# Eigenvector stage of a graph kernel: z on TensorE, the tangents' sum on GpSimd, the basis copy and each reflection's squares on ScalarE

## The reference, cut to what matters

```python
L_norm = d_inv_sqrt[:, None] * (jnp.diag(deg) - A) * d_inv_sqrt[None, :]
_, U = jnp.linalg.eigh(L_norm)
agg = jnp.einsum('mn,bnd->bmd', U.T, features)
h = jax.nn.relu(agg @ W1 + b1)
out = h @ W2 + b2
return jnp.einsum('nm,bmd->bnd', U, out)
```

## Time and profile before

| | |
|---|---|
| median of 3 runs | 1087.52 us |
| the profiled execution | 1086.33 us |
| its span | 1084.5 us |
| granted TensorE clock, mean | 0.881 of full speed |
| eigenvector stage | 38 to about 455 us, over a third of the span |

### The profile page before, as it was taken

How to read it: one execution, slowest core, us unless ns; L and a number is a source line. 1 busy time by engine, 2 the same in 40 slices (tenths; PEclk the granted TensorE clock), 3 DMA queues, 4 the chain that set the end, 5 groups by cost and what they waited for, 6 DMA issues and landing times.

```text
span 1084.5 us, 13522 instructions
## 1 busy us (share of the span) xinstructions
PE 933.4 (86%) x4093; PEld 631.0 (58%) x4093; DVE 659.7 (61%) x2237; ACT 569.2 (52%) x1460; POOL 158.8 (15%) x390
## 2 busy tenths in 40 slices
PE   4788867878866676699999999999999998899995
PEld 3555545545555565466788877886444465554443
DVE  4667676654757788357635598533544455553686
ACT  0555543754534665338655345534965565664456
POOL 0122222311322222100000000000011111110055
PEclk9699985977956555589999999999999999999998
DMA  9100000000000000000000000000000000000014
GB/s 261 32 1 1 1 1 0 1 1 1 1 1 1 1 1 1 1 1 1 1 1 1 1 2 1 2 1 1 1 1 0 0 1 1 1 0 1 0 40 116
DMA packets 14328, 12.99 MB, mean 12 GB/s; under 512 B 897, under 2 KB 11057, under 8 KB 14257
## 3 DMA queue, kind: packets, MB, share of 16 engines
q1 hardware_dynamic: 14018, 11.98, 3.9%
q10 hardware_dynamic: 238, 0.16, 0.1%
HBM read 7.89 MB, written 4.19 MB: 11 GB/s over the span
## 4 chain that ended last, share of the span: by engine, by line
PE 71%; DVE 18%; ACT 5%; issue 3%; POOL 1%; DMA 0%; DVEq 0%; SPq 0%; POOLq 0%; ACTq 0%
PE bank L884 15%; PE bank L908 9%; PE bank L805 3%; PE bank L750 3%; PE bank L740 3%; PE bank L764 3%; PE bank L795 3%; PE bank L467 2%; PE bank L573 2%; PE bank L704 2%; PE bank L460 1%; PE bank L715 1%; PE bank L871 1%; PE bank L813 1%; PE bank L863 1%
## 5 line engine op out<-in xcount | busy, mean ns | idle before, releaser
L1330 ACT ACTIVATE hid_t<-bank,gate_b 128x512 f32<-128x512 f32 (+1 forms) x252 | 150.8, 631 | 67.8 <-PE bank L908 66.7
L908 PE MATMUL bank<-ms,w_t 128*128 128x512 f32 (+1 forms) x288 | 112.9, 536 | 6.8 <-DVE ms L2062 6.8
L884 PE MATMUL bank<-hid_t,w_t 128*128 128x336 f32 (+1 forms) x296 | 106.4, 506 | 1.1 <-DVE x L2066 1.1
L1422 POOL COPY hid_t<-feat_t 128x1008 f32<-128x1008 f32 (+1 forms) x12 | 27.9, 2328 | 499.3 <-DVE feat_t L2058 499.3
L884 PE MATMUL bank<-feat_t,w_t 128*128 128x512 f32 x208 | 93.1, 603 | 0.0
L908 PEld LDWEIGHTS bank<-ms,w_t 128*128 128x128 f32 x288 | 54.6, 193 | 56.5 <-issue 34.3
L884 PEld LDWEIGHTS bank<-hid_t,w_t 128*128 128x128 f32 x296 | 56.2, 191 | 46.0 <-issue 26.2
L1124 ACT ACTIVATE hs<-bank,con 128x1 f32<-128x1 f32 x62 | 16.2, 261 | 102.3 <-PE bank L574 102.3
L1337 ACT ACTIVATE hid_t<-hid_t 128x512 f32<-128x512 f32 (+1 forms) x72 | 41.8, 580 | 52.3 <-DVE hid_t L2044 27.6
L884 PEld LDWEIGHTS bank<-feat_t,w_t 128*128 128x128 f32 x208 | 39.2, 189 | 50.9 <-issue 46.7
L982 ACT ACTIVATE x<-x,perm 128x128 f32<-128x128 f32 x128 | 52.3, 482 | 2.6 <-DVE perm L1461 2.6
(11 more groups left out here) (443 smaller groups left out, 2166.7 us busy)
## 6 DMA issues: line engine op xcount, KB each, us to landing
out<-x SPq DMA_DIRECT2D x16, 256.0 KB, 2.6
con<-in_constants SPq DMA_DIRECT2D x1, 449.0 KB, 3.2
hid_t<-in_L_gnn_W SPq DMA_DIRECT2D x2, 128.0 KB, 3.7
e_int<-in_L_gnn_src ACTq DMA_DIRECT2D x1, 128.0 KB
l_w<-in_L_gnn_W SPq DMA_DIRECT2D x2, 64.0 KB
wg<-in_L_gnn_Wg SPq DMA_DIRECT2D x2, 64.0 KB
adj_n<-in_adj SPq DMA_DIRECT2D x1, 64.0 KB, 3.7
hid_t<-in_L_gnn_W_lin SPq DMA_DIRECT2D x1, 64.0 KB, 3.3
```

Source lines behind the costliest of these rows:

```text
L884: return mm(bank[4 * u + BANK_OF[g]][:, 0:w], w_t[:, WB_IH + 4 * (it.p - 1) + g, :], lstm_x(n), start=True, stop=(it.k == 0))
L908: mm(bank[4 * u + BANK_OF[g]][:, 0:w], w_t[:, WB_HH + 4 * (it.p - 1) + g, :], lstm_h_of(it.chain)[:, 0:w], start=False, stop=True).then_in ...
L1330: f(dst[:, 0:w], bank[4 * u + BANK_OF[g]][:, 0:w], ACT.Tanh if g == G_G else ACT.Sigmoid, bias=gate_b[:, 4 * (it.p - 1) + g:4 * (it.p - 1) ...
```

## The change

Five things of the eigenvector stage move to another engine:

- z = row * sigma + y was VectorE's L1689. Now `pe_rows` leaves the accumulation of y open and a new `pe_z` adds sigma times the row with a product of a 1 x 1 weight; VectorE reads z out of PSUM. `pe_z` waits for the copied row (`h_a_row`) and for GpSimd's sigma (`h_sigma`).
- The sum of the tangents (L1637, 128 x 128) goes from VectorE to GpSimd (`pool_den`), behind GpSimd's scalars for h1.
- The copy of v_nat (`dve_v`, L1669) goes from VectorE to ScalarE, in front of the copy of v_t.
- The sum of squares of each reflection (L1720) goes from VectorE to ScalarE (`act_vector`), in front of the root.
- The square of the lead (L1115) goes from ScalarE to GpSimd.

On ScalarE, `act_vector` of h2 moves ahead of `act_y`. At the end of the program three semaphores of the final norm are replaced by counts of semaphores that exist already; the work there is the same.

```diff
+            def pe_z(h):
+                if h is None or h == HALF - 1:
+                    return
+                k = h + 1
+                pe.wait_ge(s["h_a_row"], h + 1)
+                pe.wait_ge(s["h_sigma"], h + 1)
+                mm(h_y[:, k:P], scalar(h, SIGMA), a_row[h % 2][:, k:P], start=False, stop=True).then_inc(s["h_rows"], 1)
...
                 pe_rows(h0)
                 pe_w(i)
+                pe_z(h0)
                 beside(h0)
...
                 pe_rows(h1)
+                pe_z(h1)
                 beside(h1)
...
                 pe_rows(h2)
                 pe_turn(i)
+                pe_z(h2)
                 beside(h2)
...
                 pe_rows(h3)
                 pe_y2(i)
+                pe_z(h3)
                 beside(h3)
...
             def act_vt(i, polished):
...
+                act.wait_ge(s["j_v"], i + before + polished + 1)
+                t = f(v_nat, j_v, ACT.Copy)
...
             def act_vector(h):
...
-                link(f(scalar(h, LEAD2), lead, ACT.Square, scale=2.0))
+                f(square_row[:, h + 2:P], vp_row[h % 4][:, 0, h + 2:P], ACT.Square, accum_out=scalar(h, SUM)).then_inc(s["h_sum"], 1)
                 act.wait_ge(s["h_sum"], h + 1)
+                act.wait_ge(s["h_lead2"], h + 1)
                 f(scalar(h, NORM2), scalar(h, SUM), ACT.Sqrt, scale=4.0, bias=scalar(h, LEAD2)).then_inc(s["h_norm"], 1)
...
-                act_matrix(h2)
+                act_step(h2)
                 act_y(i)
-                if h2 is not None:
-                    act_vector(h2 + 1)
...
+                pool.tensor_scalar(scalar(h, LEAD2), lead, lead, 4.0, ALU.mult, ALU.mult).then_inc(s["h_lead2"], 1)
...
+            def pool_den(i):
+                pool.wait_ge(s["j_hyp"], i + 1)
+                pool.tensor_tensor(jt, jabs, jhyp, ALU.add).then_inc(s["j_den"], 1)
...
             def dve_tangents(i):
-                dve.wait_ge(s["j_hyp"], i + 1)
-                link(tt(jt, jabs, jhyp, ALU.add))
+                dve.wait_ge(s["j_den"], i + 1)
...
-                    link(stt(z_row[:, k:P], a_row[h % 2][:, k:P], scalar(h, SIGMA), h_y[:, k:P], ALU.mult, ALU.add))
...
-                squares(h + 1)
```

More of the change, by code:

```diff
@@ L62 @@
 TILES = 2 * PAIRS
+FIN_BASE = 2 * TILES + PAIRS
 AT_TURNED, AT_PRODUCTS, AT_LEVEL, AT_Q = (1, 11), (2, 12), (3, 13), (8, 19)
@@ L259, in graph_layers @@
         c_col = hs[:, 23:24]
+        square_row = s_flt[0:1, :]
         kept, solved, wy_t, wy_n = src_1h, dst_1h[0:HALF, 0, :], dst_1h[:, 1, :], rot[0:HALF, :]
@@ L331, in graph_layers @@
             x_ready ln_var ln_std ln_scale l0_added deg_in deg_std bn_var bn_std eig_start
[L332 removed]
+            j_w j_w_sb j_vw j_off j_d j_osq j_dif j_dsq j_sign j_sum j_hyp j_den j_t j_root j_b j_bt j_x j_y j_v1 j_y_sb j_v1_sb
             j_y2 j_y2_sb j_p1 j_f j_f_sb j_v j_vt j_v_sb j_vt_sb j_vv j_m
[L334 removed]
+            h_copied h_col h_a h_a_row h_rows h_c h_sum h_norm h_sigma h_lead h_lead2 h_half h_pv h_w h_read h_rank h_kept0 h_kept1 h_kept2 h_kept3 pool_chain
             basis_pe basis_turned_sb basis_z_sb basis_n_sb basis_iso e_signs
@@ L343, in graph_layers @@
             lstm_turned lstm_gates lstm_acts lstm_c lstm_tanh lstm_h
-            fin_turned fin_added fin_var fin_std fin_scale fin_pool fin_act fin_dve stored""".split()
+            fin_turned fin_added fin_pool fin_act fin_dve stored""".split()
         s = {n: sem(n) for n in names}
@@ L562, in pe_rows @@
                 mm(h_a[:, k:P], ident[:, k:k + 1], a_sb[:, k:P], start=True, stop=True).then_inc(s["h_a"], 1)
-                mm(h_y[:, k:P], c_col, a_sb[:, k:P], start=True, stop=True).then_inc(s["h_rows"], 1)
+                mm(h_y[:, k:P], c_col, a_sb[:, k:P], start=True, stop=False)
+            def pe_z(h):
[5 more added lines that the diff above has]
+                mm(h_y[:, k:P], scalar(h, SIGMA), a_row[h % 2][:, k:P], start=False, stop=True).then_inc(s["h_rows"], 1)
             def pe_rank(h):
@@ L646, in jacobi_turn @@
                     pe_rows(h4)
+                    pe_z(h4)
                     beside(h4)
@@ L1102, in act_vt @@
                 before = sum(t < i for t in POLISHED)
+                act.wait_ge(s["j_v"], i + before + polished + 1)
+                t = f(v_nat, j_v, ACT.Copy)
+                if polished or i not in POLISHED:
+                    t.then_inc(s["j_v_sb"], 1)
+                else:
+                    t.then_inc(s["j_m"], 1)
                 act.wait_ge(s["j_vt"], i + before + polished + 1)
@@ L1340, in final_root @@
                 a_, b_ = FIN_GROUPS[g]
-                act.wait_ge(s["fin_var"], g + 1)
-                f(fin_rs[:, a_:b_, :], fin_rs[:, a_:b_, :], ACT.Sqrt).then_inc(s["fin_std"], 1)
+                act.wait_ge(s["ln_var"], FIN_BASE + g + 1)
+                f(fin_rs[:, a_:b_, :], fin_rs[:, a_:b_, :], ACT.Sqrt).then_inc(s["ln_std"], 1)
             def final_normalised(t):
-                act.wait_ge(s["fin_scale"], fin_group(t) + 1)
+                act.wait_ge(s["ln_scale"], FIN_BASE + fin_group(t) + 1)
                 for b in range(TB):
@@ L1410, in _ @@
                 pool_vw(i)
-                for h in steps_of(i):
+                for n, h in enumerate(steps_of(i)):
+                    if n == 1:
+                        pool_den(i)
                     if h is not None and h != STEPS_BEFORE - 1 and h + 1 < HALF:
@@ L1426, in _ @@
             for t in FIN_POOL:
-                pool.wait_ge(s["fin_scale"], fin_group(t) + 1)
+                pool.wait_ge(s["ln_scale"], FIN_BASE + fin_group(t) + 1)
                 for b in range(TB):
@@ L1664, in dve_f @@
                 stt(jf_sb, j_f, ROOT3, jb0, ALU.mult, ALU.add).then_inc(s["j_f_sb"], 1)
[L1666 to L1673, removed]
             def dve_half(i):
@@ L1695, in dve_reflected @@
                 dve.wait_ge(s["h_pv"], h + 1)
-                link(dve.tensor_tensor_reduce(e_vec[:, k:P], pv[:, k:P], z_row[:, k:P], 0.5, 0.0, ALU.mult, ALU.add,
+                dve.wait_ge(s["h_rows"], h + 1)
+                link(dve.tensor_tensor_reduce(e_vec[:, k:P], pv[:, k:P], h_y[:, k:P], 0.5, 0.0, ALU.mult, ALU.add,
                                               hs[0:1, 16:17]))
-                stt(w_row[:, k:P], v[:, k:P], hs[0:1, 16:17], z_row[:, k:P], ALU.mult, ALU.subtract).then_inc(s["h_w"], 1)
+                stt(w_row[:, k:P], v[:, k:P], hs[0:1, 16:17], h_y[:, k:P], ALU.mult, ALU.subtract).then_inc(s["h_w"], 1)
                 dve.wait_ge(s["h_w"], h + 1)
@@ L1744, in dve_new_row @@
                 copy(vp_row[h % 4][:, 0, h + 1:P], k_row[:, h + 1:P]).then_inc(s["h_c"], 1)
-                squares(h)
             def jacobi_turn(i):
@@ L1814, in eigenvectors @@
                 dve.sem_inc(s["h_copied"], 1)
-                squares(0)
                 tt(c_col, a_sb[:, 0:1], COL(22), ALU.mult).then_inc(s["h_col"], 1)
@@ L2084, in final_stats @@
                     link(d)
-                    ts(fin_rs[:, a_:b_, :], fin_mv[:, a_:b_, :, 1], EPS, None, ALU.add).then_inc(s["fin_var"], 1)
+                    ts(fin_rs[:, a_:b_, :], fin_mv[:, a_:b_, :, 1], EPS, None, ALU.add).then_inc(s["ln_var"], 1)
             def final_scale(g):
                 a_, b_ = FIN_GROUPS[g]
-                dve.wait_ge(s["fin_std"], g + 1)
+                dve.wait_ge(s["ln_std"], FIN_BASE + g + 1)
                 link(dve.reciprocal(fin_rs[:, a_:b_, :], fin_rs[:, a_:b_, :]))
                 stt(fin_shift[:, a_:b_, :], fin_mv[:, a_:b_, :, 0], -1.0, fin_rs[:, a_:b_, :], ALU.mult, ALU.mult)\
-                    .then_inc(s["fin_scale"], 1)
+                    .then_inc(s["ln_scale"], 1)
             def final_normalised(t):
-                dve.wait_ge(s["fin_scale"], fin_group(t) + 1)
+                dve.wait_ge(s["ln_scale"], FIN_BASE + fin_group(t) + 1)
                 for b in range(TB):
```

6 lines of the change are left out of this document (removed).

## The result

The changed kernel takes 1098.86 us, the median of 4 runs (1097.28 to 1099.58), against 1086.93 us for the kernel before (1086.25 to 1088.42, 4 runs): a ratio of 1.0108, 95% interval 1.0097 to 1.0120. The forecast was 1087.0 with a range up to 1093.5, so it was wrong by 12 us and the time lies above the range.

What follows compares the result with a forecast made beforehand. TensorE was taken as busiest, but unevenly by pass, with VectorE busier in the third. 15.8 us leave the path and 15.5 come: 1087.0 us, no measurable difference; 8-in-10 range 1080.5 to 1093.5 us.

Steps and rivals of the forecast that it cites:

- z on TensorE: TensorE's 1 x 1 products for z, 0.20 or 0.29 us each in the chain: 5.1 + 1.5 + 0.5 us come onto the path.
- My upper bound of 0.48 us: Cost per z product if priced as the first product after a wait on TensorE; it would give 9.6 us.
- the clock: Sign expected in the profile after: TensorE's granted clock in layer 0's three passes stays within 0.05.
- Rival 2: Fuller TensorE raises its clock in the third pass: 4 us gained, 1081 us with part of rival 1's relief; chance 0.08.
- What z frees on VectorE: z leaves VectorE, where it is in the chain at 16 places: 4.4 us leave the path.
- rival 4: VectorE waits for GpSimd's half as long as z took; half of 8.2 us isn't had: 1091 us, chance 0.09.
- The wait for sigma: `pe_z` holds TensorE's in-order queue until GpSimd's sigma: 0.15 us in each of 10 turns, 1.5 us.
- rival 3: TensorE's queue stalls for sigma at `pe_z`, 0.6 us in 15 turns, 6.8 us more: 1094 us, chance 0.21.
- The copy of v_nat: Moved to ScalarE: 4.0 us leave before L507 in the third pass, 1.1 us come in the second.
- The tangents' sum: Moved from VectorE to GpSimd: 2.6 us leave at 12 turns, 1.2 us come as GpSimd slows VectorE.
- the rule in the prediction: Only VectorE instructions with two SBUF inputs contend with GpSimd reading SBUF; by it the 1.2 us would be near 0.
- The squares and the order: Squares to ScalarE: 3.8 us leave, 3.6 come before the root; ScalarE doing sigma first for h2: 1.0 us leaves.

Runs made afterwards that it cites:

- e1: The changed kernel with z back on VectorE, the other four parts kept: 1074.08 us, ratio 0.9878 to the kernel before.
- e7: The kernel before, z on VectorE, plus an idle 1 x 1 product at z's place on TensorE that waits for ScalarE's copied row: 1107.10 us, ratio 1.0187.
- e2: The kernel before with z alone moved to TensorE: 1098.31 us, ratio 1.0091.
- e12: The changed kernel with z on VectorE and, at z's place on TensorE, an idle full-column product waiting for ScalarE's copied row: 1098.54 us, ratio 1.0100.
- e14: The changed kernel with z on VectorE and an idle full-column product at z's place on TensorE, without the wait for ScalarE's row: 1095.65 us, ratio 1.0078.
- e3: The kernel before with only the copy of v_nat moved to ScalarE: 1080.85 us, ratio 0.9936.
- e8: The kernel before with only the tangents' sum moved to GpSimd: 1082.99 us, ratio 0.9958.
- e11: The kernel before plus an idle 1 x 1 product inside `pe_rows`, between the row's product and y's, its result unused: 1097.68 us, ratio 1.0112.
- e6: The kernel before, z on VectorE, plus an idle 1 x 1 product without a wait at z's place, also signalling that y is ready: 1101.50 us, ratio 1.0150.
- e15: The changed kernel with z on VectorE and, at z's place on TensorE, an idle one-column product waiting for ScalarE's row: 1084.48 us, ratio 0.9973.
- e10: The changed kernel with z on VectorE in turns 5 to 10 and on TensorE in the other turns: 1084.99 us, ratio 0.9974.

## Why the prediction was wrong, point by point

**z on TensorE: the term that failed.** The forecast had 5.1 + 1.5 + 0.5 us for the product and 1.5 for the wait, 8.6 us against 4.4 us saved, so +4.2. In company it is +24.8. Three steps of it failed, and the first two are the main ones.

First, the size. I took 0.20 and 0.29 us from pieces of the chain of waits. Such a piece runs from what released it to the next link and isn't the length of the product. In the timeline the products of these two pieces take 0.36 and 0.49 us:

```profile
109.59 0.36 PE L563 MATMUL bank<-u_t,hs 128*1 128x116 f32 x2
303.39 0.49 PE L563 MATMUL bank<-u_t,hs 128*1 128x86 f32 x2
```

The group of L563, shown above, has 26.2 us for 63 products, 0.42 us each, and was there to be read. My upper bound of 0.48 us was close to the truth, and I then applied it to 20 places.

Second, the places. I counted 20 products as costly and hid the rest behind waits. The first pass did hide them, as said: 0.2 us a turn for a forecast of 0.1. But from turn 5 to turn 10 the change is 14.4 us longer than e1 for the 17 products that lie between these two marks, 0.85 us each, and from 10 to 15 8.0 us for 22, 0.36 each. That the sum nearly equals the products' whole busy time is thus partly chance: below it in one pass, above it in another.

Third, the clock. I said it would stay within 0.05 in the three passes. Against the kernel before it did, in the three stretches (0.99 to 1.00, 0.81 to 0.78, 0.53 to 0.50, where 0.5 is the lower level throughout). But the price of z was worked out at a fixed clock, and that is what fails: without z the clock rises to 0.82 and 0.61 in the second and third pass (e1; 0.80 and 0.55 before), and with z it is 0.77 and 0.51. In the turn above it fell from 1.00 to 0.90, worth some 3 us in that turn alone. Rival 2 had the clock as a possible gain; it turned the other way.

**What z frees on VectorE.** 4.4 us forecast. Up to some 10 us alone (e7 against e2) and nothing in company (e12 against the change). This is the mechanism of rival 4, named at 9%. e1, the same kernel with z on VectorE, shows it:

```profile
L1704 DVE SCALAR_TENSOR_TENSOR rows<-rows,hs,bank 1x127 f32<-1x127 f32 (+62 forms) x63 | 18.9, 299 | 24.7 <-POOL hs L1413 13.3 <-ACT rows L1152 6.2 <-PE bank L565 4.6
L1706 DVE RECIPROCAL hs<-hs 1x1 f32<-1x1 f32 x64 | 9.7, 151 | 13.9 <-POOL hs L1418 12.6
```

There z is 18.9 us of work with 24.7 us of waiting before it, and the reciprocal waits 13.9 us more, 57.5 us in all; with z gone VectorE waits 52.7 us for GpSimd's half instead. What z took came back as waiting.

**The wait for sigma, rival 3.** Its outcome (slower, 1094) was the nearest, its mechanism not. The waits for GpSimd's sigma are 2.3 us, as the forecast's "some 3 us" had it; the late piece is ScalarE's row, which `pe_z` needs as well and which the forecast put at nothing. (z on VectorE waited for it already.) In TensorE's queue the same wait is worth 2.9 us (e14), since others stand behind it.

**The copy of v_nat.** 4.0 us less 1.1 was forecast, and e3 gave 6.9. The idle time before the product of L507 over the stage, before and in e3:

```profile
L507 PE MATMUL bank<-av,lap 128*128 128x128 f32 x32 | 10.2, 412 | 6.1 <-DVE av L1669 5.4 <-ACT av L1104 0.5
```

```profile
L507 PE MATMUL bank<-av,lap 128*128 128x128 f32 x32 | 9.5, 386 | 1.7 <-ACT av L1110 1.7
```

It fell by 4.4 us, and ScalarE is next: the step was right. The loss in the second pass didn't come (+0.2 us over its five turns for 1.1). The third pass gained 9.3 us in one profile, more than the idle time and more than the 6.9 us of the runs; its clock rose with it, from 0.50 to 0.62 in its turn of 31.1 us, which took 28.4. So 6.9 for 2.9 us isn't explained by the waits alone. In the changed kernel the idle time before this product is gone too: L509 at 347.42 follows L565, and behind it z:

```profile
346.90 0.28 ACT L1125 ACTIVATE av<-bank 128x128 f32<-128x128 f32 x1
347.02 0.48 PE L565 MATMUL bank<-u_t,hs 128*1 128x81 f32 x2
347.42 0.80 PE L509 MATMUL bank<-av,lap 128*128 128x128 f32 x2
348.15 0.42 PE L573 MATMUL bank<-rows,hs 1*1 1x81 f32 x2
```

**The tangents' sum.** 2.6 less 1.2 us for GpSimd's contention were forecast; e8 gave 4.6. In the profiles 2.8 us are one turn, from 7 to 8, before and in e8, and then in e11, which has the sum on VectorE and a product more in TensorE's queue:

```profile
219.83:240.99 21.16, 16.15 (x70) 10.44 (x69) 11.23 (x42) 9.92 (x35) 3.77 (x13) 0.71 0.01 2
```

```profile
219.90:238.28 18.38, 13.59 (x71) 8.69 (x70) 10.91 (x42) 10.07 (x36) 4.33 (x14) 0.86 0.01 2
```

```profile
222.90:240.09 17.19, 12.45 (x74) 7.89 (x73) 11.22 (x42) 9.93 (x35) 3.87 (x13) 0.95 0.00 1
```

In e8 the same products took 2.6 us less of TensorE, at a clock of 0.86 instead of 0.71. But e11 has this turn still shorter, at 0.95, and e6 too (17.7 us at 0.93), so its length goes with the clock and can't be put down to the sum. The other 1.8 us fit the forecast's 1.4.

The contention itself can be read in the profiles. In e8 the addition on GpSimd lies beside VectorE's pv, which took 0.30 to 0.32 us there in 14 turns and 0.24 to 0.27 us at the same widths in the kernel before, some 0.7 us in all. In the changed kernel four of these, in the first pass, took 0.50 us, when the addition had started just before:

```profile
75.41 0.45 POOL L1430 TENSOR_TENSOR perm<-perm 128x128 f32<-128x128 f32 x1 [0.26 <-ACT perm L1098]
75.44 0.50 DVE L1705 TENSOR_SCALAR seg<-seg,hs 1x122 f32<-1x122 f32 x1
82.38 0.27 DVE L1705 TENSOR_SCALAR src_st<-src_st,hs 1x121 f32<-1x121 f32 x1
356.13 0.23 DVE L1710 CUSTOM_DVE_ANT_0 rows<-tmp,bank 1x80 f32<-1x80 f32 x1
356.40 0.28 DVE L1712 SCALAR_TENSOR_TENSOR rows<-tmp,hs,bank 1x80 f32<-1x80 f32 x1
```

All together some 1.2 us more of VectorE for the 1.2 forecast; how much of it is on the path isn't known. The inner product and w, which now read z from PSUM, weren't longer beside the addition (0.23 and 0.28 us, in the last two lines), as the rule in the prediction has it. But pv, with one row and a scalar as its input, was, so "near 0" by that rule isn't borne out.

**The squares and the order.** 3.8 + 1.0 less 3.6 us, so -1.2, were forecast, and -0.7 (interval -1.8 to +0.5) measured. (The first of the 16 pieces of L1720 in the chain is at 38.54 us, ahead of the turns, and not the one at 163.39; the sum stays about the same.) The root starts 0.37 us after the square, where 0.43 was taken from the earlier trace rows:

```profile
346.03 0.25 ACT L1135 ACTIVATE s_flt<-src_st 1x80 f32<-1x80 f32 x1
346.19 0.18 ACT L1135 ACTIVATION_READ_ACCUMULATOR s_flt<-src_st 1x1 f32 x1
346.40 0.29 ACT L1138 ACTIVATE hs<-hs 1x1 f32<-1x1 f32 x1
```

**The sum.** Without z the forecast amounts to -5.5 us and the runs to -13; with z to +4.2 and +24.8. Two errors of opposite sign made a forecast of no difference look better founded than it was. As I read it both have one root: I priced instructions by the places at which the chain happened to show them, at a fixed clock. For z the runs and rows above bear this out. For the gains of the copy and the sum it is argued from single profiles.

Of the signs named beforehand these came: no idle time before the product of L507, the root 0.37 us after the square, 2.3 us of waits for sigma for some 3. These didn't: z takes 0.39 us and not 0.2 to 0.3, the third pass is shorter by 0.3 us a turn and not by 0.5 to 1.5, and the second is longer by 2.3 us a turn.

## What to carry to other kernels

Before work is moved to the busiest engine to relieve another, take the whole busy time of a like instruction at the same count from the grouped view (here 26.2 us for L563). Where that engine is the bound, this is a better first price than a few pieces of the chain, even for a product with a 1 x 1 weight. Here it came out at 24.8 us in all, but at 0.85 us a product in one pass and under 0.2 in another. And a wait moved into its queue holds up all that stands behind. Ask what the relieved engine waits for next; here it was GpSimd, and the relief was worth nothing once other parts had shortened VectorE. And try the parts of such a change one by one: three of the four here were worth 13 us, and the fourth hid it.

## What the runs showed of the hardware

- An fp32 product of a 1 x 1 weight keeps TensorE busy for 0.39 us over 65 to 127 columns and for 0.18 us over one (24.6 and 11.6 us for 63). These lengths rest on modelled ends. I had expected next to nothing for the second.
- A `TENSOR_SCALAR` of VectorE over one row of 122 took 0.50 us beside a 128 x 128 addition of GpSimd that had started 0.03 us earlier, and 0.27 us over 121 without it (after, 75.44 and 82.38 us).
- TensorE's granted clock in a turn moved by 0.1 to 0.2 between kernels with small edits, both ways: 0.71 to 0.86 when VectorE's sum left (e8; 0.95 in e11, which keeps the sum), 1.00 to 0.90 when five products with full columns came (e12 against e15), and 0.69 to 0.50 in the turn from 11 to 12 when z was on TensorE there (e10 against e1):

```profile
310.73:337.36 26.63, 18.21 (x100) 15.02 (x101) 17.52 (x81) 12.44 (x54) 9.12 (x32) 0.69 0.01 2
```

```profile
311.63:341.07 29.44, 25.80 (x110) 19.69 (x111) 15.84 (x77) 13.00 (x54) 9.17 (x32) 0.50 0.01 2
```

In this last pair TensorE is busy for 88% of the turn at the lower clock and for 68% at the higher. So a fuller TensorE didn't bring the clock up here; which way it falls before an edit is made, no view of these traces told me.
